# Causal attention and a mixture of experts on one Trainium2 core: scores from two fp32 parts in 32-row tiles, row maxima by blocks of 128 keys

## The reference, cut to what matters

```python
# x: (4, 1024, 128), 16 heads of 8 dimensions
q = gelu(concat([q_c, rope(x @ wqr + bqr)]))       # per head 8 wide
k = gelu(concat([k_c, rope(x @ wkr + bkr)]))
scores = einsum('bhqd,bhkd->bhqk', q, k) / sqrt(8)
scores = where(causal, -inf, scores)               # 1024 x 1024 per head
attn = softmax(scores, axis=-1)
out = einsum('bhqk,bhkd->bhqd', attn, v) @ wo + bo
x = x + layernorm(out)
# then a layer of 8 experts, two per token, and a shared one
```

## Time and profile before

| | |
|---|---|
| median of 3 runs | 953.57 us (950.37 to 955.49) |
| the profiled execution | 952.68 us, its span 950.9 us |
| PE busy | 758.0 us, 80% of the span |
| VectorE busy | 633.1 us, 67% |
| ScalarE busy | 521.8 us, 55% |
| GpSimd busy | 339.2 us, 36% |
| mean granted TensorE clock | 0.89 |
| DMA | 70.23 MB, 108390 packets |

### The profile page before, as it was taken

One profiled execution on the slowest core, in us unless ns is written; L12 is line 12 of the kernel. 1 busy time (PEld: TensorE's weight loads), 2 busy tenths in 40 slices (PEclk: granted clock), 3 DMA queues, 4 the chain that ended last, 5 costly groups with the idle time before them and its releaser, 6 DMA issues. The chain is left out here.

```text
span 950.9 us, 18955 instructions
## 1 busy us (share of the span) xinstructions
PE 758.0 (80%) x5615; PEld 369.0 (39%) x5615; DVE 633.1 (67%) x1912; ACT 521.8 (55%) x1048; POOL 339.2 (36%) x510
## 2 busy tenths in 40 slices
PE   5886799999999997999999998757766019898910
PEld 2331233333333332333333332346655007787800
DVE  6898788887787874778787883136554405565647
ACT  3562367767776663776777777447534004344424
POOL 3673112231222221122222223122665744555542
PEclk9996599999999997999999999859768659999965
DMA  6469253332134312313332202332112222222263
GB/s 165 140 168 215 81 109 51 62 61 52 24 60 65 60 29 43 56 25 54 65 63 37 34 6 52 78 77 68 51 48 70 76 68 71 76 82 68 63 175 107
DMA packets 108390, 70.23 MB, mean 74 GB/s; under 512 B 43773, under 2 KB 95390, under 8 KB 108062
## 3 DMA queue, kind: packets, MB, share of 16 engines
q1 hardware_dynamic: 95440, 56.05, 28.2%
q0 software_dynamic: 4352, 8.99, 2.9%
q10 hardware_dynamic: 8498, 3.97, 1.7%
HBM read 43.59 MB, written 22.89 MB: 70 GB/s over the span
## 5 line engine op out<-in xcount | busy, mean ns | idle before, releaser
L266 DVE CUSTOM_DVE_ANT_0 x_in<-ps,mask 128x1024 bf16<-128x1024 f32 (+7 forms) x512 | 364.3, 755 | 82.1 <-PE ps L255 73.3
L736 ACT ACTIVATE expT<-ps 128x512 f32<-128x512 f32 (+1 forms) x640 | 330.5, 553 | 161.1 <-PE ps L855 143.9
L855 PE MATMUL ps<-q_space,k_space 96*128 96x512 bf16 (+3 forms) x768 | 222.7, 335 | 15.4 <-issue 6.2
L255 PE MATMUL ps<-k_space,q_space 96*128 96x512 bf16 (+3 forms) x768 | 198.9, 345 | 17.1 <-DVE mx L266 11.0
L829 PE MATMUL ps<-expT,vr 128*9 128x256 f32 (+1 forms) x2560 | 179.4, 362 | 1.2 <-POOL expT L713 1.2
L713 POOL TENSOR_SCALAR_AFFINE_SELECT expT<-expT 128x512 f32<-128x512 f32 x128 | 82.5, 657 | 235.8 <-ACT expT L736 235.8
L855 PEld LDWEIGHTS ps<-q_space,k_space 96*128 96x128 bf16 x768 | 61.1, 98 | 165.6 <-ACT expT L736 106.9
L255 PEld LDWEIGHTS ps<-k_space,q_space 96*128 96x128 bf16 x768 | 64.4, 100 | 81.9 <-DVE mx L266 44.8
L1118 POOL DMA_INDIRECT expert_rows<-rows,tile_to x72 | 68.9, 957 | 66.7 <-ACT rows L1197 45.3
L829 PEld LDWEIGHTS ps<-expT,vr 128*9 128x9 f32 x2560 | 41.7, 89 | 96.4 <-issue 60.9
L1080 POOL DMA_INDIRECT sorted_rows<-rows,places x64 | 62.2, 973 | 18.7 <-issue 18.7
(11 more groups left out here) (188 smaller groups left out, 974.8 us busy)
## 6 DMA issues: line engine op xcount, KB each, us to landing
q_space<-q_parts SPq DMA_DIRECT2D x48, 192.0 KB
rows<-sorted_rows SPq DMA_DIRECT2D x72, 65.0 KB, 1.9
k_space<-k_parts SPq DMA_DIRECT2D x32, 128.0 KB
q_parts<-parts SPq DMA_DIRECT2D x24, 128.0 KB, 2.4
k_parts<-parts SPq DMA_DIRECT2D x24, 128.0 KB, 2.7
k_space<-k_parts SPq DMA_DIRECT2D x16, 192.0 KB
v_ones<-v_st SPq DMA_DIRECT2D x8, 288.0 KB, 3.9
vr<-v_ones SPq DMA_DIRECT2D x16, 144.0 KB
```

What stands on the lines that cost most here:

```text
L255: last = nc.tensor.matmul(psw[:, at + lo:at + hi], qr[:, rr, hh, qi * P:(qi + 1) * P], kr[:, rr, hh, lo:hi], start=True, stop=True)
L266: last = nc.vector.tensor_tensor_reduce(out=unread[:, odd, col:col + width], in0=psw[:, 2 * CT * odd + col:2 * CT * odd + col + width], in ...
L736: act.activation(expT[:, (NS * r + s) % PTN, hh, 0:width], ps[:, B_S + hh % 2, 0:width], ACT.Exp, scale=SCALE).then_inc(exp_ok, 1)
L855: last = nc.tensor.matmul(ps[:, B_S + hh % 2, col:col + m], kr[:, r, hh, kt * P:(kt + 1) * P], qr[:, r, hh, q0:q0 + m], start=True, stop=True)
```

## The change

q and k are kept as two fp32 parts of rounded fp32 (F32R) in place of three bf16 parts, so a head needs 3 x 8 = 24 rows and two more for the maximum. A group's four heads stand below each other in one tile, each from row 32 * hh, and a matmul names only its head's 24 or 26 rows. GpSimd subtracts once per chunk and tensor, ScalarE's rounding is gone, the filler DMAs are replaced by one memset of the k rows; a group is loaded with 17 DMAs in place of 10.

A wide "max" item now covers two heads, one PSUM bank of four blocks of 128 keys for each, chosen by `MAX_KINDS`: nine kinds, 18 items per group in place of 24, 6 of them a group early. VectorE takes eight maxima of 128 columns with one plain reduce over the 1024 columns, and after the ninth kind one small reduce joins the blocks. The mask is no longer an operand of VectorE: in the two kinds that hold the diagonal blocks PE first writes it into the banks, with a matmul of the identity by the mask (L260 after), and the scores are added on top. The third part of the negated maximum goes, so `split_neg` has three operations in place of five. Stage three gets tiles of its own; its instructions stay.

```diff
...
-ROWS = 9 * HD
-MROWS = ROWS + 3
-KROWS = 96
-PAIR_OF_ONES = float(np.array([0x3F803F80], np.uint32).view(np.float32)[0])
+HEAD_ROWS = P // GH
+ROWS = 3 * HD
+MROWS = ROWS + 2
...
-HEAD_ITEMS = [[(7, 0)], [(3, 0), (0, CT)], [(6, 0)], [(2, 0), (1, CT)], [(5, 0)], [(4, 0)]]
-MAX_ITEMS = [(hh, tiles) for hh in range(GH) for tiles in HEAD_ITEMS]
-NM = len(MAX_ITEMS)
-EARLY = 8
-IN_ONE = 18
+SQ = QT
+MAX_KINDS = [([(qi, 0, 4, 0, 1)], qi, SQ) for qi in range(4, QT)] + [
+    ([(2, 0, 2, 0, 2), (6, 4, 2, 1, 2)], 4 * SQ + 2, 4),
+    ([(3, 0, 2, 0, 2), (7, 4, 2, 1, 2)], 4 * SQ + 3, 4),
+    ([(1, 0, 1, 0, 1), (3, 2, 1, 1, 1), (5, 4, 1, 2, 1), (7, 6, 1, 3, 1)], 6 * SQ + 1, 2),
+    ([(qi, qi, 1, qi, 1) for qi in range(4)], 7 * SQ, 1),
+    ([(qi, qi, 1, qi - 4, 1) for qi in range(4, QT)], 7 * SQ + 4, 1),
+]
+NK = len(MAX_KINDS)
+DIAG_KIND = NK - 2
+NM = 2 * NK
+EARLY = 6
+IN_ONE = 13
...
-        seq = nxt[:17] + neg[:1] + nxt[17:22] + [("out", 0, 0)] + nxt[22:] + early[:4] + neg[1:] + early[4:]
+        seq = nxt[:12] + neg[:1] + nxt[12:16] + [("out", 0, 0)] + nxt[16:] + early[:3] + neg[1:] + early[3:]
     else:
-        seq = nxt[:11] + prev + neg[:1] + nxt[11:] + early[:1] + [("out", 0, 0)] + early[1:4] + neg[1:] + early[4:]
+        seq = nxt[:5] + prev + nxt[5:7] + neg[:1] + nxt[7:] + early[:1] + [("out", 0, 0)] + early[1:3] + neg[1:] + early[3:]
...
-    qd = nc.dram_tensor("q_parts", (B, H, 3, HD, S), BF16, kind="Internal").ap()
-    kd = nc.dram_tensor("k_parts", (B, H, 3, HD, S), BF16, kind="Internal").ap()
+                 lns_d, lnb_d, gate_d, wg_d, wu_d, wd_d, swg_d, swu_d, swd_d, cos_d, sin_d, tab_d, out_d):
+
+    qd = nc.dram_tensor("q_parts", (B, H, 2, HD, S), F32, kind="Internal").ap()
+    kd = nc.dram_tensor("k_parts", (B, H, 2, HD, S), F32, kind="Internal").ap()
...
+        at3 = sb(top, "at3", [P, 2, NT, E])
+        attention = top.enter_context(ExitStack())
+        qr = sb(attention, "q_rows", [P, RING, S], F32R)
+        kr = sb(attention, "k_rows", [P, RING, S], F32R)
+        vr = sb(attention, "vr", [P, RING, QT, GH * VW])
+        mask = sb(attention, "mask", [P, CT], BF16)
+        part = sb(attention, "block_max", [P, 2, GH, QT * SQ])
+        mx = sb(attention, "mx", [P, 2, GH * QT])
...
-            qg, kg = (at_row(a, b)[r * GH:(r + 1) * GH].rearrange("h s d t -> (s d) h t") for a in (qd, kd))
-
-            for i in range(3):
-                row, end = 3 * HD * i, 3 * HD * (i + 1)
-                sp.dma_start(qr[row:end, r], qg).then_inc(group_in[r], DMA)
-                sp.dma_start(kr[row:end - i * HD, r], kg[i * HD:]).then_inc(group_in[r], DMA)
-                if i:
-                    sp.dma_start(kr[end - i * HD:end, r], kg[0:i * HD]).then_inc(group_in[r], DMA)
+            qg, kg = (at_row(a, b)[r * GH:(r + 1) * GH] for a in (qd, kd))
+            for hh in range(GH):
+                q, k = (head(a, r, hh, ROWS).bitcast(F32) for a in (qr, kr))
+                both = "i d s -> (i d) s"
+                for dst, src in ((q[0:HD], qg[hh, 0]), (q[HD:], qg[hh].rearrange(both)),
+                                 (k[0:2 * HD], kg[hh].rearrange(both)), (k[2 * HD:], kg[hh, 0])):
+                    sp.dma_start(dst, src).then_inc(group_in[r], DMA)
             sp.dma_start(vr[:, r], at_row(vd, b)[:, :, r * GH * VW:(r + 1) * GH * VW]).then_inc(group_in[r], DMA)
 
-            fill_rows(sp, qr, r, ROWS, MROWS, 0).then_inc(group_in[r], DMA)
-
-        def fill_rows(sp, a, r, lo, hi, value):
-
-            return sp.dma_start(a[lo:hi, r].rearrange("p h s -> p (h s)").bitcast(F32), const_d[value].partition_broadcast(hi - lo))
+        def head(a, r, hh, n):
+
+            return a[HEAD_ROWS * hh:HEAD_ROWS * hh + n, r]
...
         def scores_for_max(pe, odd, rr, which):
 
-            hh, tiles = MAX_ITEMS[which]
-            for qi, col in tiles:
-                width = P * (qi + 1)
-                for lo in range(0, width, CT):
-                    hi = min(width, lo + CT)
-                    at = 2 * CT * odd + col
-                    last = nc.tensor.matmul(psw[:, at + lo:at + hi], qr[:, rr, hh, qi * P:(qi + 1) * P],
-                                            kr[:, rr, hh, lo:hi], start=True, stop=True)
+            pair, kind = divmod(which, NK)
+            pieces, _, _ = MAX_KINDS[kind]
+            banks = [psw[:, CT * (2 * odd + i):CT * (2 * odd + i + 1)] for i in range(2)]
+            if kind >= DIAG_KIND:
+                for bank in banks:
+                    nc.tensor.matmul(bank, identb[:], mask[:], start=True, stop=False)
+            for n, (qi, k0, width, at, step) in enumerate(pieces):
+                for i in range(2):
+                    q, k = (head(a, rr, 2 * pair + i, ROWS) for a in (qr, kr))
+                    out = banks[i].rearrange("p (b c) -> p b c", c=P)[:, at:at + step * (width - 1) + 1:step]
+                    last = nc.tensor.matmul(out, q[:, qi * P:(qi + 1) * P], k[:, k0 * P:(k0 + width) * P],
+                                            start=kind < DIAG_KIND, stop=kind < DIAG_KIND or n == len(pieces) - 1)
             last.then_inc(wide_ready, 1)
 
         def maxima(dve, n, odd, rr, which):
 
-            hh, tiles = MAX_ITEMS[which]
-
-            wait_apart(dve, wide_used, n - 1, passed_dve)
-            for qi, col in tiles:
-                width = P * (qi + 1)
-                last = nc.vector.tensor_tensor_reduce(
-                    out=unread[:, odd, col:col + width], in0=psw[:, 2 * CT * odd + col:2 * CT * odd + col + width],
-                    in1=mask[:, S - width:], scale=1.0, scalar=NEG, op0=ALU.add, op1=ALU.max,
-                    accum_out=mx[:, rr % 2, QT * hh + qi:QT * hh + qi + 1])
-            last.then_inc(wide_used, 1)
+            pair, kind = divmod(which, NK)
+            _, first, step = MAX_KINDS[kind]
+            heads = slice(2 * pair, 2 * pair + 2)
+            nc.vector.reduce_max(part[:, rr % 2, heads, first:first + 3 * step + 1:step],
+                                 psw[:, 2 * CT * odd:2 * CT * (odd + 1)].rearrange("p (h k c) -> p h k c", h=2, c=P),
+                                 AX_X).then_inc(wide_used, 1)
+            if kind == NK - 1:
+                wait_apart(dve, wide_used, n + 1, passed_dve)
+                nc.vector.reduce_max(mx[:, rr % 2, 2 * QT * pair:2 * QT * (pair + 1)].rearrange("p (h q) -> p h q", q=QT),
+                                     part[:, rr % 2, heads].rearrange("p h (s q) -> p h q s", q=QT),
+                                     AX_X).then_inc(mx_ok, 1)
...
-                    for i in range(3):
+                    for i in range(2):
                         for which, dst in enumerate((qb, kb)):
-                            sp.dma_start(dst[:, i, :, at], parts[:, p, which, i]).then_inc(stored[p], DMA)
+                            sp.dma_start(dst[:, i, :, at], parts[:, p, which, i].bitcast(F32)).then_inc(stored[p], DMA)
...
-                        if isinstance(j, int) and j == 0:
-                            for r in (2 * p, 2 * p + 1):
-                                fill_rows(sp, kr, r, ROWS, KROWS, 1).then_inc(rows_in, DMA)
-                                fill_rows(sp, qr, r, MROWS, KROWS, 0).then_inc(rows_in, DMA)
...
-                def part_rest(c, p, i):
+                def part_low(c, p, i):
                     pool.wait_ge(gelu_ok, 4 * c + 2 * i + 2)
-                    wait(pool, mid_ok, 2 * c - 2 + i)
-                    nc.gpsimd.tensor_tensor(rest[:, p, i], full[:, p, i], parts[:, p, i, 0],
-                                            ALU.subtract).then_inc(rest_ok, 1)
-
-                def part_low(c, p, i):
-                    pool.wait_ge(mid_ok, 2 * c + i + 1)
-                    nc.gpsimd.tensor_tensor(parts[:, p, i, 2], rest[:, p, i], parts[:, p, i, 1],
+                    nc.gpsimd.tensor_tensor(parts[:, p, i, 1], full[:, p, i], parts[:, p, i, 0],
                                             ALU.subtract).then_inc(low_ok, 1)
 
                 root(0, 0)
                 root(1, 1)
+                nc.gpsimd.memset(kr[:].rearrange("p r s -> p (r s)").bitcast(F32), 1.0).then_inc(rows_ok, 1)
+                nc.gpsimd.memset(part[:], NEG).then_inc(part_ok, 1)
...
-                            part_rest(c - 1, 1 - p, 1)
-                            part_low(c - 1, 1 - p, 0)
                             part_low(c - 1, 1 - p, 1)
                         if exists(c + 2, CHUNKS):
                             root(c + 2, p)
-                        part_rest(c, p, 0)
+                        part_low(c, p, 0)
...
-                def part_mid(c, p, i):
-                    act.wait_ge(rest_ok, 2 * c + i + 1)
-                    act.activation(parts[:, p, i, 1], rest[:, p, i], ACT.Copy).then_inc(mid_ok, 1)
...
-            negs = sb(two, "negs", [P, 2, 2, 2, 3, QT], BF16)
-            negT = sb(two, "negT", [2 * 3 * QT, 2, P], BF16)
+            negs = sb(two, "negs", [P, 2, 2, 2, 2, QT])
```

(39 more changed lines are left out.)

60 lines of the change are left out of this document (19 added, 41 removed).

## The result

The changed kernel takes **1268.57 us** (1267.76 to 1270.07, 4 runs), the kernel before 953.91 us beside it: ratio 1.3307, interval 1.3267 to 1.3347. The forecast was 981 us, with 938 to 1030 as its range. The sign was right and the size far off: a third slower where 3% was forecast. The right sign owes little to the forecast's reasons, since most of the loss has a cause that it didn't have.

The account below looks back on a forecast made before the run. PE was taken as the bound, 94% of a 30.3 us group in stage two. Terms summed to +2.5 us per group, +34 over 14 groups, with -5 for stage one: 952.7 + 34 - 5 = 981 us, range 938 to 1030.

Parts of the forecast that it names:

- (a): "Max" stream on PE: paired heads run side by side, but mask matmuls eat the saving; 7.9 us per group as before, -0.
- (d): Neighbouring scores in different tiles and banks share PE, 10 of 20 pairs: -2.2 us per group, bounds -3 and 0.
- the second: Rival on PE: the second head's weight load waits for the first's, narrow pairs cost 0.11 more each; 1023 us, chance 0.20.
- third rival: On PE: the tiles don't run together at all, so shared scores and wide pairs lose their saving; 1079 us, chance 0.05.
- (b): PE weight loads left bare after returns from the product with v: +1.4 us per group; 0.3 if time goes with rows.
- (b) to (d): PE per group: bare weight loads +1.4 us, switches between whole array and quarter tiles +0.8, neighbouring scores sharing PE -2.2.
- first rival: Stage two: scores also overlap the other pair's maxima and loads hide, a group goes under 30 us; 931 us, chance 0.18.
- (e): Turn 16 holds five items, the fifth waiting for VectorE to read the third: +2.1 us per group, bounds 1 and 3.1.
- (f): VectorE: reduces at 1.15 us (bounds 1.07, 1.22), joins 0.3; 22.8 us per group for 24.2, PE waits less: -0.8.
- (g): Lumps: ScalarE sets the pace in light pairs of turns and idles in heavy ones: +1.2 us per group, bounds 0 and 2.5.
- (h): Stage one: less VectorE sharing with GpSimd -4 us, filler DMA wait gone but more SyncE issues -1; bounds -10 and +2.
- (i): Stage three: no instruction changes, 0.

## Why the prediction was right or wrong

**The step that failed** is the one under the whole sum: every PE price, (a) to (d), was taken from starts at 1.00 and multiplied by counts, and the text allowed only "the part at half clock after the loop's own pause". That the change itself could move the clock was in no term and no rival. Shown: with 32 rows and nothing else changed the clock stays at 0.50 and the time is 1299.72 us. A hint was on hand: from 88 to 125 us of the trace of before PE was busy 27.91 of 37.00 us and the clock read 0.65, so a busy PE did not have the full clock as a matter of course.

**(a) pairs and loads, right.** The heads of a pair start together: in the trace the four wide matmuls of an item start at 433.714, 433.717, 434.460 and 434.463 us. The pairs of a narrow item, too, start within 3 ns: at 442.741, 443.016, 443.229 and 443.442, from the second on 0.213 apart at 1.2 GHz, twice the 0.11 that was priced at 2.4, and their eight loads take 0.93 us in all:

```profile
442.74 0.93 PEld L265 LDWEIGHTS ps<-k_rows,q_rows 24*128 24x128 f32 x8 [0.84 <-issue]
```

So loads of two tiles run side by side; the second and the third rival are refuted. By the rule of the Trainium skill cited in the prediction ("TensorEngine Tiling (Array Packing)", Key Properties), the trace agrees. A load of 24 rows also takes what one of 128 rows does at the same clock, 0.213 us at 1.2 GHz for 0.11 at 2.4, so the case of (b) in which time goes with rows is out. The third rival's sum was off besides: 2.2, 2.6 and 3 make 7.8 per group and 1090 us, not 7 and 1079.

**(b) to (d), the operands' net of 0.0 per group**, can be measured only at 1.2 GHz: 48.55 us with tiles of rounded fp32 against 53.04 with few rows of bf16 and the same maxima, -4.5. Halved, as an estimate for the full clock, -2.2. So the overlap was probably worth more than its price. The first rival's mechanism is there: a score also shares PE with maxima (L835 starts at 421.71 us and L265 at 421.73). Whether it would have carried a group under 30 us at full clock no run shows; at 1.2 GHz PE stays the bound.

**(e) Turn 16, right in kind.** PE's timeline after:

```profile
431.95 0.79 PE L835 MATMUL ps<-q_rows,k_rows 26*128 26x512 f32 x1
432.67 1.11 PE L786 MATMUL ps<-identf,oT 128*128 128x128 f32 x4
433.71 1.54 PE L265 MATMUL ps<-k_rows,q_rows 24*128 24x512 f32 x4
436.03 0.37 PE L781 MATMUL ps<-identf,negs 128*32 128x128 f32 x1 [0.78 <-DVE block_max L274]
436.96 0.58 PE L265 MATMUL ps<-k_rows,q_rows 24*128 24x256 f32 x2 [0.56 <-DVE block_max L274]
```

The turn lasts 5.1 us (431.95 to 437.06), with PE twice behind VectorE's reduces, 0.78 and 0.56 us. At full clock, on bf16 parts, spreading it gave back 33.83 - 31.45 = 2.4 us per group (+2.1 forecast), plus the short falls of the clock that came with it and that I hadn't thought of.

**(f), (g).** A reduce takes 1224 ns on average, just above the upper bound of 1.22, and joins take 0.38 for 0.3. VectorE is busy 24.4 us per group (98.65 of 212 us, times 52.34), where 22.8 was forecast and 24.2 stood before, so its work did not shrink. On bf16 parts, where masks aren't paid for by pairing (8 x 0.22 = 1.8), my terms give 1.8 + 2.1 - 0.8 + 1.2 = +4.3 per group; measured +3.2 (33.83 - 30.65). The mask's 1.8 was measured as 1.73 and turn 16's 2.1 as 2.4, each by taking it out, so it is (f) and (g) together that were too dear: +0.4 forecast, -0.9 left (29.72 - 30.65). No run tells the two apart.

**(h) Stage one**: the first exp comes at 101.96 us for 107.57, -5.6 for -5 forecast. Its split was less good: L507 (L520 before) averages 1096 ns for 1255, -2.5 us for -4, and "under 1 us" was wrong; PE's wait at its first item fell from 3.72 to 0.42. **(i)** 0 forecast, -5.8 measured behind the last division. Part of it may be the clock, 0.81 from 940 us to the end for 0.78 from 612 us to the end before; it is not shown. The two together, -11.4, are also past the 10 us outside stage two that the prediction had named as a sign of being wrong.

Had the clock held, 33.83 and -2.2 would make 31.6 us per group, an estimate from two runs; the forecast said 32.8. By that estimate the arithmetic of the mechanisms was good to about 1 us per group, and small beside the 20.7 us (52.34 - 31.6) that the clock took.

## What to carry to other kernels

Before shrinking a matmul's contraction, ask what clock the new shape will be granted, and try it first by itself: cutting the rows read in the old kernel is a two-line edit and shows a loss as large as the whole (1299.72 us for 1268.57). Rows of zeros that look like waste may pay for themselves: without them, with 75 rows for 96, the clock came back later and the time was 976.46 us for 965.2, in one run, which points that way and doesn't show it. And PE busy at 96 to 100% with every other engine at little more than half its old share was here the sign of a slow clock, not of more work: read the clock's line beside the busy one.
